# A macaron block on one core: which engine issues the transfers of high and middle K

## What is computed

```
x = x + 0.5 * moe_ffn(layernorm(x))     # 16 experts, 2 chosen per token, SiLU gate
x = x + attention(layernorm(x))         # 16 heads of 16, causal
x = x + 0.5 * moe_ffn(layernorm(x))     # the same weights again
```

```
qkv = x @ w_qkv;  q = q / sqrt(16)
scores = einsum('bqhd,bkhd->bhqk', q, k), masked causally
attn = softmax(scores);  out = (attn @ v) @ w_out
```

## Time and profile before

| | |
|---|---|
| median of 3 runs | 804.26 us (803.93 to 809.54) |
| the profiled execution | 804.25 us |
| its span | 802.5 us |
| mean granted clock of TensorE | 0.913 |
| busy: PE, DVE, ACT, POOL | 645.4, 550.0, 385.4, 401.1 us |
| attention | about 205 to 556 us of the span |

### The profile page before, as it was taken

One profiled execution on the slowest core, in us unless ns is written; L12 is line 12 of the kernel. 1 busy time (PEld: TensorE's weight loads), 2 busy tenths in 40 slices (PEclk: granted clock), 3 DMA queues, 4 the chain that ended last, 5 costly groups with the idle time before them and its releaser, 6 DMA issues.

```text
span 802.5 us, 18544 instructions
## 1 busy us (share of the span) xinstructions
PE 645.4 (80%) x5486; PEld 524.6 (65%) x5503; DVE 550.0 (69%) x1536; ACT 385.4 (48%) x962; POOL 401.1 (50%) x466
## 2 busy tenths in 40 slices
PE   2638899998679999999999999987558999859300
PEld 2427799996446777777777777654347999748200
DVE  7877755554668888888888886764878455437542
ACT  2534466664216555555555555546624656515100
POOL 5124366664625555555555422224043777775674
PEclk9958999999879999999999999999859999969755
DMA  8883355657554444444444433301413566665754
GB/s 263 272 280 108 103 164 170 169 169 139 143 162 134 123 121 114 122 122 122 122 121 121 113 95 94 94 3 65 148 55 110 163 194 189 166 130 157 235 160 122
DMA packets 94160, 113.48 MB, mean 141 GB/s; under 512 B 11648, under 2 KB 84624, under 8 KB 94096
## 3 DMA queue, kind: packets, MB, share of 16 engines
q1 hardware_dynamic: 80240, 74.87, 29.4%
q0 software_dynamic: 13824, 37.77, 19.3%
q10 hardware_dynamic: 32, 0.02, 0.0%
HBM read 49.30 MB, written 33.55 MB: 103 GB/s over the span
## 4 chain that ended last, share of the span: by engine, by line
PE 63%; DVE 11%; POOL 8%; issue 6%; DMA 6%; ACT 3%; SPq 1%; DVEq 1%; POOLq 0%; ACTq 0%
PE bank L869 14%; PE bank L876 7%; PE bank L474 6%; PE bank L415 6%; PE bank L460 5%; PE bank L435 5%; POOL shared L706 4%; PE bank L858 4%; PE bank L422 3%; PE bank L494 3%; PE bank L438 3%; DMA spare<-normed,source 2%; POOL spare L695 2%; PE bank L482 1%; PE bank L836 1%
## 5 line engine op out<-in xcount | busy, mean ns | idle before, releaser
L695 POOL DMA_INDIRECT spare<-normed,source x128 | 126.4, 987 | 122.2 <-PE bank L858 53.4
L869 PE MATMUL bank<-xeT,shared 128*128 128x128 f32 x1280 | 175.0, 281 | 0.1
L869 PEld LDWEIGHTS bank<-xeT,shared 128*128 128x128 f32 x1280 | 161.0, 197 | 1.1 <-issue 0.5
L365 POOL TENSOR_SCALAR_AFFINE_SELECT pr<-pr 128x512 f32<-128x512 f32 x128 | 81.0, 655 | 154.7 <-ACT pr L532 154.6
L585 DVE TENSOR_REDUCE mx<-bank 128x2 f32<-128x512 f32 (+1 forms) x192 | 128.2, 688 | 28.6 <-PE bank L438 21.3
L532 ACT ACTIVATE pr<-bank 128x512 f32<-128x512 f32 x192 | 102.8, 609 | 30.5 <-PE bank L460 18.0
L876 PE MATMUL bank<-wd_sb,hid 128*128 x320 | 99.0, 392 | 19.7 <-DVE hid L1148 19.3
L1148 DVE TENSOR_TENSOR hid<-bank,silu 128x128 f32<-128x128 f32 x160 | 46.5, 291 | 95.4 <-ACT silu L989 94.7
L985 ACT COPY xeT<-bank 128x256 f32<-128x256 f32 x160 | 59.6, 372 | 66.4 <-PE bank L858 58.9
L989 ACT ACTIVATE silu<-bank 128x128 f32<-128x128 f32 x160 | 44.3, 277 | 79.5 <-PE bank L869 79.1
L706 POOL DMA_INDIRECT shared<-grouped_out,slot x64 | 62.6, 979 | 27.9 <-issue 16.6
(11 more groups left out here) (178 smaller groups left out, 1112.6 us busy)
## 6 DMA issues: line engine op xcount, KB each, us to landing
grouped_out<-shared SPq DMA_DIRECT2D x160, 128.0 KB
shared<-parts SPq DMA_DIRECT2D x154, 128.0 KB
spare<-parts SPq DMA_DIRECT2D x70, 128.0 KB
normed<-shared SPq DMA_DIRECT2D x16, 512.0 KB, 3.6
wgu_sb<-_L_ffn_gate_up_proj_dram SPq DMA_DIRECT2D x8, 512.0 KB, 8.6
out_dram<-x_sb SPq DMA_DIRECT2D x16, 256.0 KB, 2.9
x_sb<-in_L_attn_x_dram SPq DMA_DIRECT2D x3, 1024.0 KB, 10.2
wd_sb<-in_L_ffn_down_proj_dram SPq DMA_DIRECT2D x4, 512.0 KB, 8.7
```

What stands on the lines that cost most here:

```text
L365: nc.gpsimd.affine_select(out=m, in_=m, compare_op=ALU.is_ge, fill=0.0, base=0, pattern=[[0, 4], [1, P]], channel_multiplier=-1).then_inc( ...
L695: nc.gpsimd.indirect_dma_start(xe[f][r], None, normed, bass.IndirectOffsetOnAxis(source[:, j:j + 1], 0)).then_inc(arrival(f, r), 16)
L869: last = nc.tensor.matmul(bank[2 + u][:, h * P:(h + 1) * P], wgu_tile[u][:, c, h * I:(h + 1) * I], xeT[:, u, c, :], start=(c == 0), stop=( ...
```

## The change

`SP_TURN` loses its steps HI_K and MID_K. The body that issued a part's transfers in `attn_sync` becomes a function `stack(eng, kind, b)`, which takes the engine. SyncE calls it for the three parts of Q and for low K. ScalarE calls it for high K right after its copy of high K, and for middle K right after its copy of middle K. The waits in it stay as they were.

```diff
--- before.py
+++ after.py
@@ -299,7 +299,7 @@
                     (18, SCORE, 3), (19, LEFT_K, 0), (18, SCORE, 4), (18, SCORE, 5), (19, LOW_Q, 0), (18, SCORE, 6)]
         POOL_TURN = [(8, FETCH, 2), (3, MASK, 10), (3, MASK, 11), (8, FETCH, 3), (7, ROOT, 0), (9, FETCH, 0),
                      (4, MASK, 1), (4, MASK, 2), (4, MASK, 4), (4, MASK, 5), (9, FETCH, 1), (4, MASK, 7), (4, MASK, 8)]
-        SP_TURN = [(0, HI_Q, 0), (0, MID_Q, 0), (0, LOW_Q, 0), (0, HI_K, 0), (0, MID_K, 0), (0, LOW_K, 0), (-1, MAX, 0)]
+        SP_TURN = [(0, HI_Q, 0), (0, MID_Q, 0), (0, LOW_Q, 0), (0, LOW_K, 0), (-1, MAX, 0)]
 
         def batches(steps, part):
 
@@ -366,6 +366,22 @@
                                             pattern=[[0, 4], [1, P]], channel_multiplier=-1).then_inc(at["masked"], 1)
             batches(POOL_TURN, part)
 
+        def stack(eng, kind, b):
+
+            x = OF[kind]
+            ready = {HI_Q: "hi_ready", HI_K: "hi_ready", MID_Q: "mid_ready", MID_K: "mid_ready"}
+            i = {HI_Q: 0, HI_K: 0, MID_Q: 1, MID_K: 1, LOW_Q: 2, LOW_K: 2}[kind]
+            after(eng, at[ready[kind] if kind in ready else "low_ready"], 2 * b + x + 1)
+            after(eng, at["scoreT_done"], 3 * G * (b - BUFS + 1))
+            if b < BUFS:
+                after(eng, at["ones_set"], BUFS)
+                for r in range(RING):
+                    eng.wait_ge(ye_stored[r], stores(0, NE_T))
+            for slot_no in SLOT_OF[kind]:
+                dst = (qT, kT)[x][b % BUFS][slot_no:ROWS:SLOTS, :, :]
+                eng.dma_start(dst.rearrange("d (h e) n -> d h (e n)", e=2), parts[:, x, i, :])\
+                    .then_inc(at[("stacked_q", "stacked_k")[x]], 16)
+
         def attn_sync(sp):
             def part(kind, n, b):
                 if kind == MAX:
@@ -373,19 +389,7 @@
                     after(sp, at["scoreT_done"], 3 * G * (b - BUFS + 1))
                     sp.dma_start(qT[b % BUFS][ROWS:ROWS + 3, :, :], nmaxT[:, :]).then_inc(at["maxed"], 16)
                 else:
-                    x = OF[kind]
-                    ready = {HI_Q: "hi_ready", HI_K: "hi_ready", MID_Q: "mid_ready", MID_K: "mid_ready"}
-                    i = {HI_Q: 0, HI_K: 0, MID_Q: 1, MID_K: 1, LOW_Q: 2, LOW_K: 2}[kind]
-                    after(sp, at[ready[kind] if kind in ready else "low_ready"], 2 * b + x + 1)
-                    after(sp, at["scoreT_done"], 3 * G * (b - BUFS + 1))
-                    if b < BUFS:
-                        after(sp, at["ones_set"], BUFS)
-                        for r in range(RING):
-                            sp.wait_ge(ye_stored[r], stores(0, NE_T))
-                    for slot_no in SLOT_OF[kind]:
-                        dst = (qT, kT)[x][b % BUFS][slot_no:ROWS:SLOTS, :, :]
-                        sp.dma_start(dst.rearrange("d (h e) n -> d h (e n)", e=2), parts[:, x, i, :])\
-                            .then_inc(at[("stacked_q", "stacked_k")[x]], 16)
+                    stack(sp, kind, b)
             batches(SP_TURN, part)
 
         def attn_tensor(pe):
@@ -506,10 +510,14 @@
                     after(act, at["qk_done"], 2 * b + x + 1)
                     after(act, at[("stacked_q", "stacked_k")[x]], 16 * SLOTS * b)
                     nc.scalar.copy(parts[:, x, 0, :], (bankB, bankA)[x][:, :]).then_inc(at["hi_ready"], 1)
+                    if kind == HI_K:
+                        stack(act, HI_K, b)
                 elif kind in (MID_Q, MID_K):
                     x = OF[kind]
                     after(act, at["left_ready"], 2 * b + x + 1)
                     nc.scalar.copy(parts[:, x, 1, :], left[:, x, :]).then_inc(at["mid_ready"], 1)
+                    if kind == MID_K:
+                        stack(act, MID_K, b)
                 elif kind == V:
                     after(act, at["v_done"], b + 1)
                     after(act, at["pv_done"], G * (b - 1))
```

## The result

| | before | changed |
|---|---|---|
| median | 805.11 us (803.93 to 809.54, 4 runs) | 820.66 us (818.60 to 823.41, 4 runs) |
| ratio | | 1.0201, 95% interval 1.0169 to 1.0233 |
| profiled execution | 804.25 us | 823.41 us |
| its span | 802.5 us | 821.7 us |

The change makes the kernel 2.0% slower: 15.6 us by the medians, where 9.65 were forecast. In the changed kernel the lines have moved: the issues of the transfers are L382, high K's copy L512, middle K's L518, the exponentials L540, the T matmuls L464, the V matmuls L426.

A forecast was written before the change was run, and what follows sets the result against it. TensorE was taken to bound the kernel, each microsecond it waits in a pass costing one. High K 9.4, pass 2 +2.15 and the start -1.9 sum to +9.65 us, so 813.9 us, in a range of 807 to 823.

The forecast's parts named there:

- High K, passes 3 to 15: Three issues before the first exponential make it 0.91 us late; TensorE waits 0.72 us a pass, 9.4 us over 13 passes.
- the lead of 0.19: Before T 3 in each pass: it starts at 427.04 but could start at 426.85, so 0.19 us of lateness is covered.
- nothing is given back: Behind T 3, TensorE has no spare time later in the pass to catch up, so the 0.72 us stays lost.
- the third rival: Two or three of ScalarE's 80 issues last up to 1655 ns behind high K, adding 1.1 us each: 816 to 817 us.
- Pass 2 and the start: Pass 2: table load and first exponential later, +2.15 us. Start of attention: batch 0's scores at 225.6 instead of 227.50, -1.9 us.
- landing times stay: Transfers at the start and after: same bytes and engines, DMA share 0.42, so they land as before; cost nothing.
- The one risk that the forecast named here: TensorE stands 2.1 us rather than 0.68 before batch 1's Q matmul; at the lower clock level 3.7 us more, 817.6.
- Middle K: Two issues behind its copy fit in 0.6 us of cover before the next ScalarE instruction: nothing lost; without cover, up to 1.2 us a pass.
- One issue at a time: Rival: SyncE and ScalarE cannot issue together, so 13 x 0.95 = 12.4 us come on top, 826.3 us; chance 0.12.
- Hidden issues: Rival: three issues of up to 0.36 us each fit before the first exponential, 13 passes cost nothing, 802.4 us; chance 0.10.
- the upper end: Forecast's high end: at 0.746 us an issue, 13 x 1.20 = 15.6, 2.6 and -1.2 give 821.3 us.

The follow-up runs named there:

- The stand-in: Kernel before, no transfer moved; from batch 3 ScalarE does three copies into an unused tile behind the copy of high K: 814.82 us, 1.0112.
- the change again: The changed kernel run once more beside the kernel before: 820.89 us, 1.0203.
- high K alone: Against the changed kernel, middle K's issues go back to SyncE and ScalarE issues only high K: 820.02 us, 1.0176 of the kernel before.
- two issues: Against the changed kernel, ScalarE issues two of high K's three transfers, SyncE the rest and middle K: 864.27 us, 1.0046 of the kernel before (859.88 on that chip).
- middle K alone: Against the changed kernel, high K's issues go back to SyncE and ScalarE issues only middle K: 802.65 us, 0.9968 of the kernel before.
- batch 0 alone: Against the changed kernel, ScalarE issues high and middle K of batch 0 only, SyncE all others: 857.69 us, 0.9974 of the kernel before (859.88 on that chip).
- the first four experiments: Four kernels on one chip beside the kernel before: the change again 820.89 us, high K alone 820.02, middle K alone 802.65, the stand-in 814.82.
- middle K alone, again: The kernel in which ScalarE issues only middle K and SyncE high K, run once more: 803.28 us, 0.9984 of the kernel before.

## Why the prediction came out as it did

The forecast was 813.9 in a range of 807 to 823; 820.66 was measured. The mechanism held and its size was short: 9.65 us were forecast, 15.6 came by the medians and 19.2 in the profiled execution.

**High K, passes 3 to 15: right in place, mis-sized.** The step forecast a first exponential 0.91 us late, a lead of 0.19 and 0.72 us a pass, 9.4 in all. It is 1.02 late and costs 0.90, 11.7 in all. Three issues took 1.90 us for 1.86; 0.1 us are the exponential's own semaphore checks behind the issues, which nothing hides any more; and the lead of 0.19 was misread. A row of the chain starts where the matmul before it ends, and neighbouring matmuls overlap, so 427.04 is not T 3's start. In the timeline the next score starts at 427.10, and it follows T 3 by 0.23 us in the changed kernel (441.25 to 441.48), so T 3 started at about 426.88, only 0.03 behind the prediction's 426.85. And "nothing is given back" was wrong: T 3 slips by 0.99, the pass by 0.90. So the 0.18 us that the forecast was short are 0.11 of lateness and 0.16 of lead, less 0.09 given back. The stand-in shows that the lateness alone does this.

**Long issues: the third rival came true on top, at its price, and brought a cost that it did not name.** In the profiled run three third issues stood on the chain:

```profile
288.75 1.45 ACTq L382
...
332.10 1.55 ACTq L382
...
374.51 2.11 ACTq L382
```

They belong to high K of batches 4, 6 and 8. Against 0.62 they are 0.83, 0.93 and 1.49 us longer, and those passes are longer than 20.74 by 0.83, 0.92 and 3.13. The issues' own 3.25 us are what the prediction gave for three (1.1 each). SyncE has such issues too, but there nobody waits. They come back at the same batches: the change again has them in 4 and 6, high K alone in 4 and 8 (1.16 and 1.61 us). What lengthens them is open; no run told it apart. The rest of the 3.13 is the clock. TensorE stood 2.28 us before T 3 in that pass, and 2.07 us in pass 2, and behind both the granted clock fell to 0.51 for 3.4 us, from the upper level of 2.4 GHz to the lower of 1.2:

```profile
247.70:251.00 3.30, 3.30 (x21) 2.10 (x23) 2.23 (x4) 1.89 (x4) 2.41 (x4) 0.51 0.02 5
...
377.40:380.80 3.40, 3.40 (x21) 2.51 (x22) 1.38 (x3) 2.25 (x5) 1.86 (x3) 0.51 0.13 37
```

In batch 8's pass that cost 3.13 - 1.49 = 1.64 us; the pauses of 1.6 and 1.7 us in two other passes brought no fall. In the traces of the change again and of high K alone the 2.06 us pause of pass 2 was followed by the lower level as well, in the second for about 7 us. The length of the pause does not settle it: with two issues, one of 1.41 us in pass 2 was followed by 3.4 us at 0.50 (251.6 to 255.0). This step was missing. The prediction thought of the clock at the start alone, for one pair of matmuls.

**Pass 2 and the start: the sum up to T 3 came out near by luck, and the clock behind it was missing.** Here are TensorE, then ScalarE's issues and the copy behind them, and the DMA share in two windows:

```profile
221.29 3.72 PE L419 MATMUL bank<-anT,wqk 128*128 128x256 f32 x16 [1.58 <-ACT anT L507]
226.50 0.38 PE L439 MATMUL bank<-shared 112*128 112x128 bf16 x4 [1.49 <-DMA shared<-parts]
...
247.07 0.39 PE L464 MATMUL bank<-shared 115*128 115x256 bf16 x2 [2.07 <-ACT pr L540]
```

```profile
216.19 2.02 ACTq L382 DMA_DIRECT2D shared<-parts  x3
...
218.90 1.22 ACTq L382 DMA_DIRECT2D shared<-parts  x2
...
220.64 0.59 ACT L507 COPY anT<-bank 128x512 f32<-128x512 f32 x1
```

```profile
218.50:220.50 2.00, 1.21 (x5) 0.65 (x3) 2.00 (x7) 0.71 (x2) 0.26 (x1) 0.52 1.03 265
220.50:222.50 2.00, 1.21 (x6) 1.08 (x7) 0.95 (x4) 0.73 (x2) 1.47 (x2) 1.00 1.11 267
```

The Q and K matmuls of batch 1 moved from 220.42 to 221.29, where 221.8 was forecast, and the scores from 227.50 to 226.50, where 225.6 was. They still wait 1.49 us for transfers. The sentence that landing times stay was wrong here: the DMA share is 1.03 and 1.11 in these windows, where it was 0.79 and 0.76, and the last landing that the scores waited for was at 226.48, 5.8 us behind the start of low K's last issue at 220.67, instead of 3.35.

So the scores gained 1.0 us of the 1.9 forecast. The next 1.07 came from a term that the forecast had at nothing. Before, the 3.36 us wait was followed by the lower clock level from about 227.0 to 236.4; the changed kernel has the upper level from its first scores to T 0. TensorE in that stretch, before and changed (columns as in the earlier trace rows):

```profile
227.00:246.00 19.00, 15.71 (x79) 10.09 (x82) 14.90 (x32) 5.02 (x9) 1.74 (x2) 0.74 0.43 124
```

```profile
226.50:243.70 17.20, 12.87 (x79) 8.16 (x79) 14.71 (x32) 4.27 (x8) 1.90 (x3) 1.00 0.44 127
```

From the first scores to T 0 it is 18.29 us before (227.50 to 245.79) and 17.22 changed (226.50 to 243.72), so T 0 comes 2.07 us earlier. The other traces fit: with no low stretch in between it is 17.2 to 17.3 us (middle K alone, batch 0 alone), with about 3 us of it 17.3 to 17.8 (five traces), with about 6 us 18.3 to 18.5 (three). No run held the transfers fixed and changed the clock alone. In pass 2 the issues and the checks put 1.93 us between the copy of high K and the table load (243.19 to 245.12), where 2.15 was forecast. T 3 starts at 247.07 against 247.25, -0.2 for a forecast of +0.25. The lower clock behind that pause then took 1.6 us, so that batch 2's V matmuls came 1.4 us late. The Trainium skill, DMA: Bandwidth & Descriptors, section "Issuing engines are not separate DMA queues", says that such transfers run on the same engines and interleave; this start agrees with it, with shares about 1.

The one risk that the forecast named here, batch 1's Q and K matmuls at the lower level, did not come in the change (3.72 us). It came in part where batch 0 alone was moved (5.41 us).

**Middle K: right.** Its cover stood; the idle time before the PV copy is 1.82 us in every pass shown here.

**One issue at a time: did not happen.** SyncE's high and middle Q take 3.19 us for five (436.11 to 439.30) while ScalarE begins beside them at 438.60, against 3.18 before; in these 0.7 us ScalarE's first issue takes 0.59. ScalarE's median is 621 ns against 586 on SyncE. At 0.95 us a pass for this rival alone, a pass would have been 21.5 us; it is 20.74, and all of it is in the table of lateness. The section "DMA Instruction — HWDGE (DVE, Sync)" of the Trainium skill's Perfetto Trace Analysis speaks of one block, locked for exclusive use, for two sequencers; for ScalarE and SyncE this trace does not show a wait for it. **Hidden issues** holds for one issue and fails for two: by the table a pass grows once the exponential starts 1.11 to 1.17 us behind the copy, where the prediction had 1.20.

**The sum** for the profiled run: 11.7 (13 x 0.90), 3.2 (long issues), 1.6 (clock in batch 8's pass), 1.4 up to batch 2, together 17.9 of 19.2 us. The last 1.3 lie behind batch 15 (289.9 us against 288.6), where nothing was changed and where this stretch took 288.8 to 291.4 us in the traces of the first four experiments. The forecast's sum had 9.4 for the first term, 0.25 for the last, the long issues only as a rival, and nothing for the clock behind a pause. 820.66 lies inside the range, but what carried it into the upper half is not what the upper end stood for, an issue of 0.746 us.

## What to carry to other kernels

An engine that is idle 40% of the time can still be on the path at one place in a pass. Before instructions are put on it, the idle time to read is the one directly behind the new place, less what its next instruction is ahead of its user; here 1.0 us, room for one issue of 0.6 and not for three. The same issues later in ScalarE's list, in a wait of 2.57 us, are free, long ones too.

Transfers that only arrive earlier than their user needs them gain nothing; look for the pass where the user waits, here the first. A chain row's start is where the row before it ends; when overlapping instructions leave a lead of tenths, read the starts in the timeline.

## What the runs showed of the hardware

An issue of this pattern (16 partitions, 8 runs of 1 KB each) holds ScalarE for 0.62 us in the median and SyncE for 0.59, and now and then ScalarE for 1.2 to 2.1 us and SyncE for up to 1.9 (1.68 in the kernel before, 1.90 in middle K alone, again). Pauses of TensorE of 2.06 to 2.28 us, four in three traces, were each followed by the lower clock, mostly for some 3.4 us, which cost 1.6 us more. Of shorter ones, those of 1.6 and 1.7 us in the change were not, and one of 1.41 us with two issues was. In the change again the level also fell (233.7 to 236.4) behind two pauses of 0.7 us at 231 and 232.8; the same two in the change brought no fall. So no run here gives a safe length of a pause.
